# Attention with a shared rotation of three PSUM double banks, and K copies on ScalarE

## The reference

```python
c_q = x @ W_DQ;  c_kv = x @ W_DKV                     # 1024 -> 256
Q = concat(c_q @ W_UQ, rope(c_q @ W_QR))              # 16 heads, 64 + 32
K = concat(c_kv @ W_UK, rope(x @ W_KR) for each head) # 64 + 32
V = c_kv @ W_UV                                       # 16 heads, 64
scores = clip(Q @ K.T, -80, 80), causal
attn = softmax(scores / sqrt(96)) @ V
x = layernorm(x + attn @ W_O)
h = gelu(x @ q8(W_fc).T + b_fc + lora) @ q8(W_proj).T + b_proj + lora
out = layernorm(x + h)
```

## Time and profile before

| what | value |
|---|---|
| median of 3 runs | 2281.96 us (2281.38 to 2328.77) |
| the profiled execution: time | 2279.72 us |
| its span, slowest core | 2278.2 us |
| spans of the 8 cores | 2270.0 to 2278.2 us |
| mean granted TensorE clock of each core | 0.758 to 0.764 |
| matmul busy | 1346.7 us, 59% |
| VectorE busy | 1061.6 us, 47% |
| ScalarE busy | 844.7 us, 37% |

### The profile page before, as it was taken

How to read it: one execution, slowest core, us unless ns; L and a number is a source line. 1 busy time by engine, 2 the same in 40 slices (tenths; PEclk the granted TensorE clock), 3 DMA queues, 4 the chain that set the end, 5 groups by cost and what they waited for, 6 DMA issues and landing times.

```text
span 2278.2 us, 28273 instructions; the slowest of 8 cores (2270.0 to 2278.2 us)
## 1 busy us (share of the span) xinstructions
PE 1346.7 (59%) x7027; PEld 681.6 (30%) x7038; DVE 1061.6 (47%) x1381; ACT 844.7 (37%) x1165; POOL 83.5 (4%) x136
## 2 busy tenths in 40 slices
PE   0073666665766666444442233324889898898885
PEld 0020122222222222111110011113556574565654
DVE  2257587777677777764455744443111201101012
ACT  0000255555555555413353045553423324233231
POOL 0000000000000000000000000000000000000000
PEclk9575788878788788657755565556899898898987
DMA  6500021121211112412220022321000000000000
GB/s 181 134 29 0 10 58 53 57 59 46 64 58 45 63 48 94 150 45 84 65 66 23 5 71 84 83 88 47 19 1 20 20 1 20 8 13 19 1 19 19
DMA packets 49661, 112.28 MB, mean 49 GB/s; under 512 B 12528, under 2 KB 23280, under 8 KB 47200
## 3 DMA queue, kind: packets, MB, share of 16 engines
q0 software_dynamic: 14912, 54.53, 7.8%
q1 hardware_dynamic: 23936, 32.60, 4.9%
q10 hardware_dynamic: 10656, 23.34, 3.6%
HBM read 97.47 MB, written 8.39 MB: 46 GB/s over the span
## 4 chain that ended last, share of the span: by engine, by line
PE 41%; DVE 24%; ACT 15%; DMA 12%; issue 7%; DVEq 1%; ACTq 1%; SPq 0%; POOLq 0%
PE PSD L314 29%; DVE CL L674 5%; PE PSD L658 4%; DMA QSG<-wPRr 4%; ACT PT L680 4%; ACT QSG L781 3%; DVE MXW L546 3%; PE PS L314 3%; DMA QSG<-wFCr 3%; PE BIG L588 3%; DVE CL L667 2%; DVE KH L509 2%; ACT QTI L785 2%; DMA STG<-xT 1%; ACT TSQ L1159 1%
## 5 line engine op out<-in xcount | busy, mean ns | idle before, releaser
L680 ACT ACTIVATE PT<-CL 128x1024 bf16<-128x1024 f16 (+1 forms) x320 | 310.7, 971 | 287.8 <-DVE CL L667 125.7
L314 PE MATMUL PSD<-XT,RTF 128*128 128x256 bf16 x2048 | 306.3, 299 | 121.8 <-ACT HH L1107 119.8
L658 PE MATMUL PSD<-QH,KH 96*128 96x512 bf16 (+3 forms) x640 | 214.1, 424 | 146.1 <-DVE CL L667 105.4
L674 DVE TENSOR_SCALAR CL<-PSD 128x1024 f16<-128x1024 f32 x192 | 235.2, 1225 | 76.3 <-PE PSD L658 54.8
L314 PE MATMUL PSD<-HH,RTP 128*128 128x256 bf16 x2048 | 236.4, 274 | 54.3 <-DVE UPt L1124 54.3
L314 PEld LDWEIGHTS PSD<-XT,RTF 128*128 128x128 bf16 x2048 | 194.9, 105 | 195.1 <-issue 139.1
L314 PEld LDWEIGHTS PSD<-HH,RTP 128*128 128x128 bf16 x2048 | 196.2, 98 | 85.7 <-issue 56.4
L588 PE MATMUL BIG<-PT,VP 128*65 128x512 bf16 (+3 forms) x640 | 202.4, 402 | 24.0 <-ACT PT L680 24.0
L1107 ACT ACTIVATE HH<-PSD,BFCS,SML 128x256 bf16<-128x256 f32 x256 | 144.3, 563 | 141.8 <-PE PSD L314 121.6
L781 ACT ACTIVATE QSG<-QSG,SML 128x512 f32<-128x512 f32 x128 | 104.0, 813 | 212.2 <-DMA QSG<-wPRr 73.4
L794 DVE TENSOR_TENSOR QSG<-QSG,QTI 128x512 f32<-128x512 f32 x128 | 88.6, 693 | 120.4 <-ACT QTI L785 115.5
(11 more groups left out here) (148 smaller groups left out, 1359.5 us busy)
## 6 DMA issues: line engine op xcount, KB each, us to landing
STG<-wFCr POOLq DMA_DIRECT2D x32, 512.0 KB, 4.8
STG<-wPRr POOLq DMA_DIRECT2D x32, 512.0 KB, 4.6
STG<-xT SPq DMA_DIRECT2D x8, 1024.0 KB, 6.8
QSG<-wFCr POOLq DMA_DIRECT2D x32, 256.0 KB, 3.0
QSG<-wFCr ACTq DMA_DIRECT2D x32, 256.0 KB, 2.8
QSG<-wPRr POOLq DMA_DIRECT2D x32, 256.0 KB, 3.2
QSG<-wPRr ACTq DMA_DIRECT2D x32, 256.0 KB, 2.7
out<-OST SPq DMA_DIRECT2D x64, 128.0 KB, 1.9
```

The lines of the kernel that those rows point to most:

```text
L314: e.matmul(outap, la, ra, start=st, stop=sp),
L658: e.matmul(self.PSD[pslot][:, 512 * half: 512 * half + qext], self.KHB[b][0:96, 128 * kt:128 * kt + 128], self.QHB[b][0:96, qlo:qlo + qext ...
L674: e.tensor_scalar(self.CLB[cs][:, 0:qw], self.PSD[pslot][:, 0:qw], 80.0, -80.0, ALU.min, ALU.max),
L680: etok = P.s(lambda e, cs=cs, qw=qw: e.activation(self.PTB[cs][:, 0:qw], self.CLB[cs][:, 0:qw], AF.Exp, scale=ISQ), waits=[ctok, self.pv_t ...
```

## The change

Three things are changed, all in phase 2. PSUM banks 4 and 5 become a third double bank, `PSD[2]`. Score pairs and production steps both draw a running number g (`rot_g`) in the order in which they are emitted, take the double bank g % 3, and wait for the instruction that emptied it for g-3 (`slot_free`): the clip of a pair, or the cast of a production step, which uses only the first half of its double bank. And the cast of K goes from VectorE to ScalarE. At the phase's end all six `ps_free` entries are set from the last three turns.

```diff
         self.PSD = [nc.alloc_psum_tensor("PSD%d" % i, [128, 1024], F32)
-                    for i in range(2)]
...
+                    for i in range(3)]
...
+    def slot_wl(self, g):
+        if g >= 3:
+            return [self.slot_free.get(g - 3)]
+        return [self.ps_free[2 * (g % 3)], self.ps_free[2 * (g % 3) + 1]]
...
         def k_step(nb):
             def go():
-                pf = self.prod_free
+                g = self.rot_g
+                self.rot_g += 1
+                sl = 2 * (g % 3)
                 mmtok = self.mmg(
-                    self.PSB[5][0:64, 0:512],
+                    self.PSB[sl][0:64, 0:512],
                     [(self.WUK[:, D * l + DH * h: D * l + DH * h + DH],
                       self.CKV[:, 2048 * l + 512 * nb: 2048 * l + 512 * nb + 512])
                      for l in range(2)],
-                    [self.ckv_r, self.wuk_r, pf] + guard)
-                kev = P.v(lambda e, b=b, nb=nb: e.tensor_copy(
+                    [self.ckv_r, self.wuk_r] + self.slot_wl(g) + guard)
+                kev = P.s(lambda e, b=b, nb=nb, sl=sl: e.copy(
                     self.KHB[b][0:64, 512 * nb:512 * nb + 512],
-                    self.PSB[5][0:64, 0:512]), waits=[mmtok] + guard)
-                self.prod_free = kev
+                    self.PSB[sl][0:64, 0:512]), waits=[mmtok] + guard)
+                self.slot_free[g] = kev
...
                 pj = (ti + idx) // 2
-                pslot = pj % 2
+                g = self.rot_g
+                self.rot_g += 1
+                pslot = g % 3
...
                     if half == 0:
-                        if pj >= 2:
-                            w.append(clip_pair.get(pj - 2))
-                        else:
-                            w += [self.ps_free[2 * pslot],
-                                  self.ps_free[2 * pslot + 1]]
+                        w += self.slot_wl(g)
...
                 clip_pair[pj] = ctok
+                self.slot_free[g] = ctok
```

More of the change, by code:

```diff
@@ L266, in __init__ @@
         self.PSD = [nc.alloc_psum_tensor("PSD%d" % i, [128, 1024], F32)
-                    for i in range(2)]
-        self.PSB = [self.PSD[0][:, 0:512], self.PSD[0][:, 512:1024],
-                    self.PSD[1][:, 0:512], self.PSD[1][:, 512:1024]] + \
-            [nc.alloc_psum_tensor("PS%d" % i, [128, 512], F32) for i in (4, 5)]
+                    for i in range(3)]
+        self.PSB = [self.PSD[i][:, 512 * hh:512 * hh + 512]
+                    for i in range(3) for hh in range(2)]
         self.ps_free = [None] * 6
@@ L491, in go @@
                      for l in range(2)],
-                    [self.cq_r, self.wuq_r, pf] + guard)
-                qev = P.s(lambda e, b=b, nb=nb: e.copy(
+                    [self.cq_r, self.wuq_r] + self.slot_wl(g) + guard)
+                qev = P.s(lambda e, b=b, nb=nb, sl=sl: e.copy(
                     self.QHB[b][0:64, 512 * nb:512 * nb + 512],
-                    self.PSB[5][0:64, 0:512]), waits=[mmtok] + guard)
-                self.prod_free = qev
+                    self.PSB[sl][0:64, 0:512]), waits=[mmtok] + guard)
+                self.slot_free[g] = qev
                 prod["q"] = qev
@@ L732, in phase2 @@
         self.last_sc = last_sc
-        for j in range(2):
-            pj = ti // 2 - 1 - j
-            self.ps_free[2 * (pj % 2)] = clip_pair[pj]
-            self.ps_free[2 * (pj % 2) + 1] = clip_pair[pj]
-        self.ps_free[5] = self.prod_free
+        for j in range(3):
+            g = self.rot_g - 1 - j
+            self.ps_free[2 * (g % 3)] = self.slot_free[g]
+            self.ps_free[2 * (g % 3) + 1] = self.slot_free[g]
     def quant_setup(self):
```

11 lines of the change are left out of this document (7 added, 4 removed).

## The result

The changed kernel takes 2224.87 us (median of 8 runs, 2221.01 to 2227.89) where the kernel before took 2281.36 (8 runs beside it). The ratio is 0.9754, with a 95% interval of 0.9743 to 0.9765: faster by 2.5%, 56 us. The forecast was 2211 us, 71 us less than before: the direction and the range hold, the forecast gain was a quarter too large. Disturbed executions are left out of every ratio in this document, though not of the medians. The profiled execution took 2221.61 us; its slowest core is core 7.

What follows compares the result with a forecast made beforehand. VectorE leads in attention, partly waiting, while TensorE waits for PSUM banks. 15 heads at 4.1 us (62), head 15 (1) and head 0 (7.6) give 71 us off 2279.7: 2209, or 2211 on the median's scale; range 2188 to 2246.

Steps and rivals of the forecast that it cites:

- Q part: Pairs 2 to 5 of a head, where Q is produced: score pair S6 starts 1.64 us sooner, clock left at 0.50.
- clock up (2201): Rival case listed only among the chances: TensorE's clock up, kernel at 2201 us; chance 0.17.
- K part: Pairs 6 to 9 of a head, where K is produced: 1.8 us more gained by the mid-head reductions; bounds 0 to 3.2.
- chain over ScalarE eats the whole gain: Rival: scores wait for K copies queued behind exps, K term falls to 0, 2238 us; chance 0.20.
- Middle: From the mid-head reductions on: S12 no longer waits behind them, VectorE loses three gaps before clips S12 to S14, 0.7 us.
- 4.1 us a head: Sum per head, 1.64 + 1.8 + 0.7; for 15 heads 62 us.
- Head 0's production: Head 0's Q and K, produced ahead of everything: with three banks 7.6 us sooner, between 4 and 9.
- Head 15: The head without production: it gets three banks and its middle wait goes, about 1 us.
- later stages: Stages after attention: they keep their code and take the same time.
- wait at the head's start: S2 waits 3.39 us for the clip of S0; it stays, since q0 uses up the third bank; nothing booked.
- Slower by the clock in the K part: Rival: clock sinks to 0.50 at S8, S9, S10 and S12, 27 us slower, 2309 us; chance 0.05.
- The signs: Attention to about 877 us, 38.5 us a head; wrong with VectorE idle before second-half clips or K-part clock at 0.50.

Runs made afterwards that it cites:

- experiment 3: Kernel before, with production alternating between its own banks 4 and 5, scores keeping two double banks, and K casts on ScalarE: 2196 us, ratio 0.962.
- experiment 1: Changed kernel with the K casts back on VectorE, so the shared rotation alone: ratio 0.982, 41.1 us a head.
- experiment 5: Changed kernel with each production step emitted right behind its pair's scores, so its cast stands ahead of that pair's exp: 2187 us, ratio 0.960.
- experiment 2: Kernel before, with only the K casts moved to ScalarE: ratio 0.990, 41.0 us a head.
- experiment 4: Kernel before, with production alternating between banks 4 and 5 and K casts staying on VectorE: ratio 0.984, 41.0 us a head.

## Why the prediction was right, and where it was off

**What bounds the kernel: right in the main.** VectorE's work and the waits for PSUM banks set the pace. But the size of a TensorE wait says little of its worth: the 105.4 us for masked clips are nearly all still there in experiment 3 (97.4), which is 3.8% faster.

**Q part, 1.64 us: right.** Over heads 1 to 14 S6 starts 1.61 us sooner after the reductions, and experiment 1 gives it to the rotation (1.65). S3 came 0.96 us sooner as replayed (forecast 1.0). The two example heads alone would say 2.3 us (S6 11.86 us after the reductions began, where it was 14.18), because up to S6 the example of the earlier trace rows was 0.4 us longer than the mean head of before, and the example after 0.3 us shorter than its mean. The forecast left the clock at the 0.50 of before (702 to 704, where a pair of score matmuls took 1.03 us). The chances also name a case "clock up (2201)"; no run shows the 10 us that it takes off the forecast. What the runs showed is that the granted clock over the scores S6 averages 0.97 where it was 0.75, and the stretch 662 to 664 of the example has it at 0.72 already:

```profile
662.00:664.00 2.00, 2.00 (x10) 0.82 (x9) 1.46 (x2) 1.17 (x3) 0.00 (x0) 0.72 0.00 0
```

S6 is no earlier for it than forecast.

**K part, 1.8 us: too large.** It is 1.3 us, and this is the term of the sum that was most in error. The chain over ScalarE was named, and its idle times are those of the replay: before the clip of S8 VectorE idles 1.13 us (replayed 1.1), and TensorE before S8, S9 and S10 0.83, 0.57 and 1.34 us (about 1.0). What the replay left out stands one pair earlier. Its list of waits has none for k0, but k0 takes the bank that q3 had, and the cast of q3 is late: k0 waits 1.22 us at 666.16 (14.1 us in all, once a head), S7 stands behind it, and VectorE idles 0.88 us before the clip of S7 on average, where it had 0.11. In experiment 5 and with own banks both this wait and this idle time are gone. The rival that the chain over ScalarE eats the whole gain was partly true, and experiment 5 shows that its price can be had back.

**Middle, 0.7 us: right in kind, 0.5 in size.** 0.5 measured here, 0.5 in experiment 1, 0.8 from the other side in experiment 3. S12's wait of 3.85 us became 0.24, and was worth only this, as said.

**4.1 us a head: 3.4.** Of the 0.7 us that are missing, 0.5 are the K part's, 0.2 the middle's and 0.1 the head's end. Times 15 that is 11 us of the 14 that are missing in the sum. The replay gave 21.3 us from reductions to reductions and 15.5 from there to the last clip, and the kernel has 21.36 and 15.59; the first agreement is luck in part, for the replay began from a head with a Q part 0.4 us longer than the mean and left out 0.5 us in the K part.

At the head's end the changed kernel falls to a granted clock of 0.50, where the one before had 1.00. A stretch of the kernel after, then one of before:

```profile
688.00:690.00 2.00, 1.88 (x5) 0.56 (x5) 0.79 (x1) 1.69 (x2) 0.00 (x0) 0.50 0.00 0
```

```profile
736.00:738.00 2.00, 1.22 (x6) 0.50 (x6) 0.66 (x1) 1.62 (x2) 0.00 (x0) 1.00 0.00 0
```

The six PV matmuls there take 2.42 us, with the next head's first scores behind them at 0.50 too (690 to 692):

```profile
688.07 2.42 PE L597 MATMUL BIG<-PT,VP 128*65 128x512 bf16 x6 [0.54 <-ACT PT L688]
690.48 1.23 PE L665 MATMUL PSD<-QH,KH 96*128 96x512 bf16 x4
```

It cost little: 2.66 us from the last clip to the next reductions, where it was 2.57.

**Head 0's production, 7.6 us: 8.0. Head 15, 1 us: 1.1.** Both close to what was said.

**The later stages, 0: they took 3.5 us more** (1331.7 us from the last denominators on, 1328.2 before, slowest cores) with the same code. In the profiled executions of the experiments this part takes 1328.6 to 1334.7 us on the slowest core, but 1355 in experiment 2 and 1365 in experiment 4, with no pattern that I could find, so I count the 3.5 us as scatter; the cause stays open.

The sum on the slowest cores of the two profiled executions: heads 1 to 14 took 602.7 us and take 554.6, 48.1 less; the first scores start 8.8 us sooner (8.0 of it head 0's production); head 0's scores 3.7, head 15 1.1. Together 61.7, less 3.5 = 58.2 us, the difference of the two spans; between the medians it is 56.5.

**The wait at the head's start, booked at nothing: right.** 3.39 before, 3.50 in the example after. **Slower by the clock in the K part: did not happen.** Over the scores S7 to S9 of heads 1 to 14 the granted clock averages 0.99 to 1.00, over those of S10, behind 1.34 us of idle time, 0.90. Before, it was 1.00 in 716 to 720, on both sides of the 1.34 us that TensorE idled ahead of 718.37. **The signs.** VectorE waits for no scores in the second half: its idle times before the clips S12 to S19 are 0.85 us in all, 0.11 each. Attention ends at 888 us and not at 877, and a head takes 39.6 us and not 38.5. Idle times of 0.83 and 0.57 us before S8 and S9 thus left the clock at 0.99 to 1.00 in the K part. At the head's end it does fall, to 0.50 in the example, but there the matmuls wait for exps (0.57 us at 686.73, 0.54 us at 688.07) and not for banks.

**The rotation.** The rotation alone brought a head from 43.0 to 41.1 us (experiment 1). With the same six banks, one rotation for groups that different engines empty gave 2225 us, a rotation for each kind 2196.

## What to carry to other kernels

Give producers whose results different engines evacuate their own rings of PSUM banks, or emit the producer and its short evacuation ahead of the long operation in the evacuating engine's queue; a shared ring ties each kind to the other's slowest queue (2.1 us of a 39.6 us head here, and either cure brought it back). Judge a wait by what the engine that sets the pace does meanwhile: S12's wait of 2.7 us in mid-head (experiment 3) belongs to a half that is only 0.8 us longer than without it, and moving VectorE's 2.5 us of side work off the head's start brought 2.3. When a change is replayed, list every wait of every step, also those that cost nothing before: k0's wait for the cast of q3 was such a one. And hold the terms against means over many heads: a comparison of two example heads put the Q part at 2.3 us where it is 1.6.
